# Two-layer graph network on one core: second-layer rows as two float32r parts, counts widened on ScalarE, all tiles summed densely

## The reference, cut to what matters

```python
edge_index = stack([src, dst])
h = maximum(layernorm(x), 0)
# layer one: each edge carries h[src] @ weight[type].T, summed at dst
x = x + segment_sum(einsum('ni,roi->rno', h, weight)[type, src], dst) + bias0
h = maximum(layernorm(x), 0)
# layer two: another self edge per node, symmetric normalisation
deg = segment_sum(1, dst)                    # with the added self edges
norm = rsqrt(deg)[src] * rsqrt(deg)[dst]
x = x + leaky_relu(segment_sum(norm * (h @ W)[src], dst) + b, 0.2)
```

## Time and profile before

| | |
|---|---|
| runs | 2443.53 us median of 3 (2439.99 to 2445.37) |
| profiled execution, span | 2849.6 us |
| first and last gather of layer one start | 74.9 and 2591.4 us in the profiled execution |
| PE, DVE, ACT, POOL busy | 82%, 43%, 46%, 59% of the span |

### The profile page before, as it was taken

How to read it: one execution, slowest core, us unless ns; L and a number is a source line. 1 busy time by engine, 2 the same in 40 slices (tenths; PEclk the granted TensorE clock), 3 DMA queues, 4 the chain that set the end, 5 groups by cost and what they waited for, 6 DMA issues and landing times.

```text
span 2849.6 us, 45882 instructions
## 1 busy us (share of the span) xinstructions
PE 2338.5 (82%) x15616; PEld 1739.1 (61%) x15616; DVE 1215.3 (43%) x3492; ACT 1320.0 (46%) x3283; POOL 1693.0 (59%) x1754
## 2 busy tenths in 40 slices
PE   2357677777887888888888999999999999989887
PEld 2356666666666666666666666666666666656345
DVE  8345556556556565555555222222222222222228
ACT  5336655565656566565666343434344343433000
POOL 4666666656656666666666666666666666662530
PEclk9578888888999999999999999999999999999999
DMA  8335446545555655656556455545454454543665
GB/s 278 90 100 154 146 156 183 159 148 170 187 173 178 193 170 185 189 175 201 174 168 205 146 160 157 160 145 167 137 157 146 138 155 143 156 134 86 200 177 170
DMA packets 325692, 464.38 MB, mean 163 GB/s; under 512 B 61414, under 2 KB 252822, under 8 KB 325462
## 3 DMA queue, kind: packets, MB, share of 16 engines
q0 software_dynamic: 83168, 228.90, 28.3%
q1 hardware_dynamic: 198198, 149.60, 17.5%
q10 hardware_dynamic: 44096, 82.95, 7.8%
HBM read 352.28 MB, written 109.01 MB: 162 GB/s over the span
## 4 chain that ended last, share of the span: by engine, by line
PE 70%; issue 11%; ACT 7%; DVE 4%; another core or an unknown queue 3%; ACTq 1%; DMA 1%; POOL 1%; DVEq 0%; POOLq 0%; SPq 0%
PE ps_slot L1556 24%; PE ps_slot L1630 15%; PE ps_proj L1587 13%; PE ps_aux L1630 11%; PE ps_slot L1601 6%; ACT staging_f L1202 2%; ACT gap_f L1257 2%; ACT onehot_f L1265 1%; ACT acc_f L1188 1%; DVE hots_f L1435 1%; DVE acc_f L1478 1%; DVE acc_f L1483 1%; DVE acc_f L1475 1%; DVE hots_f L1432 1%
## 5 line engine op out<-in xcount | busy, mean ns | idle before, releaser
L1058 POOL DMA_INDIRECT rows_f<-table,idxT x1617 | 1565.3, 968 | 904.8 <-issue 404.4
L1556 PE MATMUL ps_slot<-onehot_f,rows_f 128*128 128x128 f32 x6468 | 916.1, 295 | 138.7 <-issue 71.9
L1556 PEld LDWEIGHTS ps_slot<-onehot_f,rows_f 128*128 128x128 f32 x6468 | 864.4, 207 | 188.8 <-issue 125.7
L1257 ACT ACTIVATE gap_f<-iota,keyT 128x128 bf16<-128x128 bf16 x1617 | 529.4, 394 | 91.8 <-issue 44.8
L1202 ACT ACTIVATE staging_f<-ps_slot 128x400 bf16<-128x400 f32 x768 | 348.0, 500 | 479.7 <-remote 228.7
L1265 ACT ACTIVATE onehot_f<-gap_f 128x384 f32<-128x384 bf16 x539 | 278.4, 516 | 560.2 <-remote 349.0
L1630 PE MATMUL ps_slot<-abuf_f,stash_f 128*128 128x512 bf16 x1890 | 457.6, 387 | 51.0 <-issue 48.8
L1432 DVE TENSOR_TENSOR hots_f<-iota_m_f,key_e_f 128x400 bf16<-128x400 bf16 x768 | 279.1, 363 | 455.2 <-PE ps_slot L1601 234.3
L1630 PE MATMUL ps_aux<-abuf_f,stash_f 128*128 128x512 bf16 x1710 | 410.9, 390 | 20.4 <-issue 19.5
L1587 PE MATMUL ps_proj<-w0t,acc_f 128*128 128x256 f32 x1600 | 389.7, 394 | 20.0 <-issue 19.2
L1346 DVE TENSOR_TENSOR acc_f<-ps_slot,acc_f 128x256 f32 (+1 forms) x561 | 232.0, 414 | 404.6 <-remote 220.8
(11 more groups left out here) (159 smaller groups left out, 816.4 us busy)
## 6 DMA issues: line engine op xcount, KB each, us to landing
abuf_f<-counts_d SPq DMA_DIRECT2D x120, 640.0 KB
rows_f<-table,idxT POOLq DMA_INDIRECT x1683
stash_f<-table SPq DMA_DIRECT2D x20, 960.0 KB
table<-hs_f SPq DMA_DIRECT2D x50, 192.0 KB
table<-xres SPq DMA_DIRECT2D x10, 640.0 KB, 7.6
x_d<-x_f SPq DMA_DIRECT2D x50, 128.0 KB
acc_f<-x_d SPq DMA_DIRECT2D x50, 128.0 KB, 2.2
xt_f<-in_x_dram SPq DMA_DIRECT2D x48, 128.0 KB
```

The source lines that it names most:

```text
L1058: eng.indirect_dma_start(rows0[:, k, c, :], None, V["table0"], bass.IndirectOffsetOnAxis(ap=idxT[:, n * LOT + c:n * LOT + c + 1], axis=0)) ...
L1257: last = eng.activation(gap[:, n % 2, c, :], iota[:, :], ACT.Abs, scale=-1.0, bias=V["key"][:, n * LOT + c:n * LOT + c + 1])
L1556: last = eng.matmul(o[:, b * W:(b + 1) * W], rows0[:, k, c, b * P:(b + 1) * P], onehot[:, n % HOTS, c, :], start=(c == 0), stop=(c == LOT ...
```

## The change

* Layer two's rows are kept as two float32 words instead of three bf16 parts: `hi`, rounded by writing it as float32r, and the rest, written as float32r too (`hs`, `table1`: 512 float32, 2 KB per row where there were 1.5 KB). Stage d and `r1` are gone.
* The matmuls of `dense` take float32r operands: 10 per piece of a five-tile batch, not 15.
* The counts stay bf16 in memory; ScalarE widens them to float32r before their use (`widen`), a tile of 128x512 at a time, into a ring of eight (`wide`).
* All 50 tiles are counted and summed densely: 800 windows (768 before), 13 groups, the last of two tiles. `sum_second`, its gathers, `onedst` and the units with the identity are gone.
* Batches are now nine of five tiles, one of two (tiles 45, 46) and one of three (47 to 49).
* There is one buffer of counts during counting, two up to the last lot, four after; a buffer is free once it has been widened.
* Layer two's weights and bias are loaded after the last lot, into `acc`'s space.
* The residual add of `close` is GpSimd's, behind its gathers; `yy` and `hh` have four buffers.

```diff
-EARLY_GROUPS = 8
+EARLY_GROUPS = 6
+STAGED_GROUPS = 3
+BATCHES = (5, 5, 5, 5, 5, 5, 5, 5, 5, 2, 3)
+WIDE = 8
+WIDEN_AHEAD = 2
...
-    table1 = nc.dram_tensor("table1", (T * P, DF3), bf16).ap()
+    table1 = nc.dram_tensor("table1", (T * P, 2 * DF), f32).ap()
...
-            while (half or todo or selfs) and pe + 1.6 <= limit and len(self.pieces.get(n, ())) < (2 if n < self.tail + self.tlot else 4):
+            while (half or todo) and pe + 1.2 <= limit and len(self.pieces.get(n, ())) < (2 if n < self.tail else 4):
...
-                pe += 3.2 if self.units[-1][0] >= 0 else 0.7
+                pe += 0.1 + 0.45 * BATCHES[self.units[-1][1]]
...
+        for i, (u, t) in enumerate(self.wide):
+            free = self.last_slot[self.wide[i - WIDE][0]] if i >= WIDE else 0
+            slot = max(slot, free, self.first_slot[u] - WIDEN_AHEAD)
+            self.widen.setdefault(slot, []).append(i)
...
+            allowed = 1 if n < self.counts_end + 4 else 2 if n < self.nlot + 4 else 4
+            buf = min(range(allowed), key=lambda i: last.get(i, -1))
...
-            for m in range(PL.tlot):
-                k = m % RING1
-                eng.wait_ge(s_pe, PL.nlot + max(m - RING1 + 1, 0))
-                for c in range(LOT):
-                    eng.indirect_dma_start(rows1[:, k, c, :], None, table1,
...
+            for k in range(T):
+                eng.wait_ge(s_lk, k + 1)
+                eng.wait_ge(s_xi[k % NOUT], 16 * (k // NOUT + 1))
+                if k >= NOUT:
+                    eng.wait_ge(s_o[k % NOUT], 16 * (k // NOUT))
+                eng.tensor_tensor(zz[:, k % NOUT, :], hh[:, k % 4, :], xin[:, k % NOUT, :], ALU.add).then_inc(s_z, 1)
...
             def load_counts(u):
...
+                before = PL.count_before[u]
+                if before is not None:
+                    eng.wait_ge(s_wide, PL.wide_first[before] + BATCHES[PL.units[before][1]])
...
-                eng.activation(hs[:, t % 2, DF:2 * DF], r1[:, :], ACT.Copy).then_inc(E["mid"], 1)
+                eng.activation(hs[:, t % 2, DF:DF2], x_home(t), ACT.Relu, scale=ab[:, 0:1], bias=ab[:, 1:2]).then_inc(E["h32"], 1)
+                eng.wait_ge(E["h32"], t + 1)
+                eng.activation(hs[:, t % 2, 0:DF].bitcast(f32r), hs[:, t % 2, DF:DF2], ACT.Copy).then_inc(E["hi"], 1)
...
+            def widen(i):
+
+                u, t = PL.wide[i]
+                if i >= WIDE:
+                    v, q = PL.wide[i - WIDE]
+                    if q == BATCHES[PL.units[v][1]] - 1:
+                        eng.wait_ge(s_dn, piece_no(v, 1) + 1)
+                    else:
+                        eng.wait_ge(s_used, PL.used_first[v] + q + 1)
+                eng.wait_ge(s_ab[PL.count_buf[u]], 16 * PL.count_turn[u])
+                counts = counts_of(u)[:, :, t * HW:(t + 1) * HW]
+                eng.activation(wide_of(i, u).rearrange("p (h c) -> p h c", c=HW), counts, ACT.Copy).then_inc(s_wide, 1)
...
+                eng.tensor_tensor(hs[:, t % 2, DF:DF2].bitcast(f32r), hs[:, t % 2, DF:DF2], hs[:, t % 2, 0:DF], ALU.subtract).then_inc(E["lo"], 1)
...
-                    for t in range(BATCH):
-                        for p in range(3):
-                            last = eng.matmul(o, stash[:, k % 2, t, p * DF + half * P:p * DF + (half + 1) * P],
-                                              abuf[:, dense_no[u] % 2, :, t * HW:(t + 1) * HW], start=(t == 0 and p == 0), stop=(t == BATCH - 1 and p == 2))
...
+                for t in range(m):
+                    w = PL.wide_first[u] + t
+                    if half == 0:
+                        eng.wait_ge(s_wide, w + 1)
+                    for p in range(2):
+                        last = eng.matmul(o, stash[:, k % 2, t, p * DF + half * P:p * DF + (half + 1) * P].bitcast(f32r), wide_of(w, u),
+                                          start=(t == 0 and p == 0), stop=(t == m - 1 and p == 1))
+                    if half == 1 and t < m - 1:
+                        last.then_inc(s_used, 1)
```

529 lines of the change are left out of this document (228 added, 301 removed).

## The result

Before 2444.45 us median of four runs (2439.99 to 2446.79), after 2346.78 us, four runs too (2345.93 to 2355.93): a ratio of 0.961, 95% interval 0.959 to 0.963. The kernel is 98 us faster; 131 us were forecast. One thing has to be said before traces are compared: the experiments ran on several chips of the same kind, and two of them are slower: before takes 2817 or 2815 us there instead of 2444 us (15% more), the changed kernel 2741 us instead of 2347 us (17% more). The profile shown ahead of the prediction has the same trait. So each experiment is compared with before, or with the changed kernel, as they ran on such a chip. I call these the pausing chips and the others the quiet ones; what the traces show of the pauses stands with the experiments. Before was never profiled on a quiet chip, so how its time there is shared out between the lots and the rest is worked out, not read.

A forecast was written before the change was run, and what follows sets the result against it. The prediction took the gathers to bind the runs' lots almost wholly. Its terms, 28 + 12 + 90 us, and 1 us for other edits made 131 us off 2443.5 us, about 2312 us, range 2215 to 2395 us.

The forecast's parts named there:

- What bounds the kernel: In the lots of the timed runs: bound almost wholly by GpSimd's gathers, 1647 x 1.26 = 2075 us.
- Term 1: In the lots: dense work on TensorE falls by 194 us, of which 28 us was taken as gain.
- recording: Across the whole span: profiling was taken to lengthen the gap between gathers, the runs being 406 us shorter than the profile.
- Terms 2 and 3: Behind the last gather: TensorE catching up with the gathers, 12 us, and a shorter stretch after the last lot, 90 us.
- float32r: In TensorE's dense matmuls: 216 ns for 512 columns, the same as bf16.
- case 4: In dense matmuls: float32r takes two column times, making the kernel slower, 2670 up to 2750 us; chance 0.09.
- Case 3: Before dense matmuls: longer float32 weight loads show, 108 ns each, and the time is 2440 us; chance 0.04.
- Case 2: Lots gain nothing as gathers hold the pace, and DMA stretches the tail: 2360 to 2410 us; chance 0.12.
- Case 1: TensorE bounds the runs' lots too: up to 194 us gained there instead of 28, down to 2146 us; chance 0.10.
- Case 5: ScalarE's queue blocks, waiting widenings holding up one-hots and evacuations: 2587 us if 2 us show per unit; chance 0.05.
- GpSimd's add: In the closes: 256 elements take between 0.45 and 0.97 us, off the chain while below 0.9 us.
- The price of a close: In the 26 closes at the end: 1.05 us each, 27 us in all; bounds 0.9 and 1.32 us.

The follow-up runs named there:

- kernel of four closes and earlier buffers: Changed kernel with two leftover units taking count buffers 0 and 1 and up to four closes in a slot instead of two: 2339.2 us, 0.956 of before.
- the high part alone: Changed kernel with one part in the dense matmuls instead of two, the rows' low part left out: 2696.7 us on a pausing chip, 0.958 of before.

## Why the prediction was right, and where it was off

The sign, the order of size and the mechanism of the largest term held: 2347 us against 2312 us, inside the range; 98 us were won where 131 us were forecast. Its steps in turn:

**What bounds the kernel.** "The gathers are the floor" was right, but the floor was sized too low. I took 1.26 us a gather from single rows, 2075 us in all. The changed kernel's stretch is 2117.6 us with only 13 us of waits for TensorE in it. The mean gather is longer than most (978 ns, median 946, the longest 4.5 us): without the waits (1582.0 + 479.5)/1617 = 1.275 us from one to the next, 24 us more than I had; the waits are 13 us, and 35 look-ups instead of 30 another 6 us:

```profile
L1069 POOL DMA_INDIRECT rows_f<-table,idxT x1617: 942/946/4506, 75.7 to 2192.4; - x180
```

Of the 36 us by which the runs of before seemed to lie above the floor, some 24 us were thus this error, if a gather costs before the same. (The profiled execution is 9 us above the median, so these are upper values.)

**Term 1, 28 us, is the step that failed on the pausing chips.** It gave nothing there: with 1150 instead of 3120 dense matmuls between lots the last gather moved by 2.7 us on the same chip, and with the changed kernel whole the term was a loss of 18 us. On the quiet chip its worth was not measured; the next paragraph bounds it, by an estimate, to between 1 and 24 us. One reason is in the plan: 30 pieces of 3.24 us and 41 of 2.37 us are both 97 us in 50 slots of the stretch after counting, so cheaper matmuls were filled up with more of them and TensorE's load there stayed. The reason given for the 406 us between profile and runs ("recording") was wrong too, and with it the reading of "remote" as TensorE's waits.

**Terms 2 and 3, 12 + 90 us.** Behind the last gather before's profile has 257.2 us, the forecast for the change was 154 us, measured were 160.3 us: 97 us instead of 102 us, if before's 257 us hold on the quiet chip. They may not: the changed kernel has 168.2 us on the pausing chip, 8 us more, and before's second gather has 15.4 us of pauses. Taking both off leaves 234 us, and of the 98 us won the stretch behind the last gather would have 74 us and the lots 24 us; with the 257 us as they stand it has 97 us and the lots 1 us. In pieces, as TensorE's rows have them: TensorE ends 12.6 us behind the last gather (forecast 10); the projections 17.5 us (18.4); 5.4 us of waiting for the leftover units' counts that no step had; the leftover pieces and the two-tile batch 32 us (32); the three-tile batch with 24 closes 55 us (59); 26 closes 25 us (27); the end 12.7 us (7.5). The wait and the end, 5 us each, and the catching up, 3 us, are about half offset by the batch and the closes. The end is longer because TensorE runs ahead: VectorE starts its last close at 2342.96 us, 2.1 us behind TensorE's last row, and GpSimd's last adds wait for their loads of `x1` until 2346.2 us. The kernel of four closes and earlier buffers wins the wait back and 3 us of the end.

Of the 33 us that are missing, 28 us are term 1 and 5 us the rest if before's 257 us hold; how they are shared out is open by these 23 us.

**float32r** was taken at bf16's 0.216 us and costs 0.237 us: the lower bound was nearly right, case 4 fell. On 300 matmuls behind the lots this is 6 us, and the run with 2-byte operands shows 7 us in its time and 8 us behind its last gather. **Case 3** fell: the weight load lasts 190 ns against 99 ns before and is hidden under the matmul. **Case 2**, "the lots gain nothing, and the tail less", was half right: the lots gained nothing on the pausing chips and at most some 24 us, by the estimate above, on the quiet one, the tail most of its term. I had given it 0.12; the row that should have raised it was the mean of 968 ns beside the 0.95 us of single gathers in the earlier trace rows. **Case 1** fell with the high part alone, and the 98 us leave it no room on the quiet chip. **Case 5** fell: TensorE waited for widenings 7.5 us in all, 5.4 us of them behind the last projection; only with every widening doubled did ScalarE hold the lots back.

**GpSimd's add** was taken as free below 0.9 us; it takes 0.74 us and is not free: it makes the leaky operation on VectorE 0.16 us longer on average. The price of a close came out right (1.08 against 1.05 us) for a wrong reason, which is luck.
